# A four-layer graph network on one core: the last two products of sage_second as one of 256 columns

## The chip, the cores and the metric

The kernel runs on one core of a Trainium2 chip. Its time is the device time of one execution in microseconds (us). Three runs of the kernel before took 5426.86, 5427.26 and 5435.87 us; their median is 5427.26.

## The reference

The input is a graph of 50000 nodes with 128 features each and 100000 edges (25000 random ones in both directions, and a loop at each node). Four layers follow one another, each with a residual and a layer norm: a graph convolution, a three-layer GraphSAGE, an attention with a gated update, and a last convolution. The change touches the second and the third sum of GraphSAGE:

```python
def sage(h, w_self, w_neigh, b):
    agg = jax.ops.segment_sum(h[src], dst, num_segments=n) * inv_deg
    return h @ w_self + agg @ w_neigh + b
h = jax.nn.relu(sage(features, ws0, wn0, b0))
h = jax.nn.relu(sage(h, ws1, wn1, b1))
h = sage(h, ws2, wn2, b2)
```

All arrays are fp32. The last layer's mean over neighbours can be taken after the product with `wn2`, since both are linear. So the kernel multiplies the rows of the second layer's output with `ws2` and with `wn2` at once, stores the second product (128 features a node, table `t_v`) for the sums of the next stage, and the first one, with the residual, the bias and the node's own share added, in `r2`.

## The kernel before

The nodes are cut into 98 groups of 512 (four blocks of 128). Each stage of the network is a block of its own, with a barrier behind it, and goes once over all groups. In each stage every engine has a list of steps with a lag in groups (`over_groups`), so the order of an engine's instructions is written out by hand; the engines meet through semaphores. SP issues loads and stores, POOL the gathers of neighbours' rows. Per-edge sums are products with one-hot matrices.

In `sage_second` (lines 1695 to 1826) TensorE's order in each step is `sums` of one group, `across` of the group before it and `down` of the one before that. `sums` gives the neighbours' sums of 256 features in two banks of PSUM (helper line 910: short products, with the rows split into a high and a low part). `across` (line 1747) is the second layer: 16 products of 512 columns into banks 4 and 5, features on partitions. ScalarE's `relu` (line 1774) takes them to `hid`. `down` (line 1759) is the change's place: for each of the two weights, each of four blocks of 128 nodes and each half of the 256 features, one product with 128 rows of `hid` as the stationary operand and 128 columns of `wuv_s` as the moving one, so 32 products. `wuv_s` holds `ws2` in its columns 0 to 127 and `wn2` in columns 128 to 255. The product with `ws2` fills bank 6, block after block, that with `wn2` bank 7. Before `down` TensorE waits until both banks have been read for the group before (semaphores `kept` and `added`).

Behind `down`, ScalarE's `keep` (line 1783) copies bank 7 to `vout`, which SP stores in `t_v`. VectorE's `rest` adds bank 6 and the residual `xin` into `rout` (line 1811), adds the bias (line 1814), and then, when `kept` is there, four times `vout` times the node's own share (line 1821); SP stores `rout` in `r2`. In each step VectorE's order is: index copy for a later gather (`aim`, line 839), one-hots (874) and low parts (881), the neighbours' mean (1795, 1802), `rest`. ScalarE's order is: high parts (869), `relu`, `keep`.

`sage_first` (from line 1588) has a dense step like the new one: for each block one product of 256 columns with each of two weights, in turn, into the halves of a bank (lines 1631 and 1633), for each of four blocks, followed by eight transposes (1643).

Of the kernel before, what the change touches and what calls it, by code (L numbers as in the profile page):

```python
# [14 lines left out]
ALU = mybir.AluOpType  # L15
ACT = mybir.ActivationFunctionType
AX_X = mybir.AxisListType.X

P = 128
D = 128  # L20
HID = 256
NODES = 50000
EDGES = 100000
BLK = 4
# [160 lines left out]
def build_program(nc, x, src, dst, w1, b1, w2, b2, ws0, wn0, sb0, ws1, wn1, sb1, ws2, wn2, sb2,  # L185
# [66 lines left out]
    wuv_s = sb("wuv_s", [P, 2, HID])  # L252
# [15 lines left out]
    bank = [top.enter_context(nc.psum_tensor(f"bank{i}", [P, 512], F32)) for i in range(8)]  # L268
# [1426 lines left out]
    def sage_second():  # L1695


        with ExitStack() as ctx:
            ph = Phase(ctx, "s2")
            e = EdgeRows(ph, t_h, HID, split=True)  # L1700
            scale_row = ph.pair("scale", [P, GRP])
            xin = ph.pair("x", [P, GRP])
            ht, agg = ph.pair("ht", [P, 2, GRP], n=4), ph.pair("agg", [P, 2, GRP])
            hid = ph.pair("hid", [P, 2, GRP])
            vout, rout = ph.pair("vout", [P, GRP]), ph.pair("rout", [P, GRP])
            loaded, loaded_s, loaded_x = ph.sems("loaded", 4), ph.sems("loaded_s"), ph.sems("loaded_x")
            agged, link, link2 = ph.sem("agged"), ph.sem("link"), ph.sem("link2")
            hidden, relued, lowered = ph.sem("hidden"), ph.sem("relued"), ph.sem("lowered")
            kept, added, rested = ph.sem("kept"), ph.sem("added"), ph.sem("rested")
            st_v, st_r = ph.sems("stored_v"), ph.sems("stored_r")  # L1710
            block = ctx.enter_context(nc.Block())

            @block.gpsimd
            def _(pool):
                e.fetch(pool)

            @block.sync
            def _(sp):
                def loads(q):
                    load(sp, q, ht[q.r][:, :, :].rearrange("p h g -> p (h g)"), slab_of(htt, q.t), loaded[q.r],  # L1720
                         hidden, 4)
                    load(sp, q, scale_row[q.u][:, :], row_of(inv_d, q.t), loaded_s[q.u], agged)

                over_groups(sp, [
                    (0, loads),
                    (2, lambda q: load(sp, q, xin[q.u][:, :], own_group(t_x1, q.t), loaded_x[q.u],
                                       rested)),
                    (3, lambda q: store(sp, q, group_of(t_v[0:NPAD, :], q.t), vout[q.u][:, :], kept, st_v)),
                    (3, lambda q: store(sp, q, group_of(r2, q.t), rout[q.u][:, :], rested, st_r))])
                all_stored(sp, st_v, st_r)  # L1730

            @block.tensor
            def _(pe):
                def sums(q):
                    e.fetched(pe, q)
                    if not is_first(q.t):
                        pe.wait_ge(agged, q.t - 1)
                    e.sum_by_feature(pe, q, [bank[2 * q.u], bank[2 * q.u + 1]]).then_inc(e.summed, 1)

                def across(q):  # L1740
                    pe.wait_ge(agged, q.t + 1)
                    if not (isinstance(q.t, int) and q.t < 1):
                        pe.wait_ge(relued, q.t)
                    for o in range(2):
                        for k, (w, r) in enumerate(((ws1_s, ht[q.r]), (wn1_s, agg[q.u]))):
                            for h in range(2):
                                last = pe.matmul(bank[4 + o][:, :], w[:, h, o * P:(o + 1) * P], r[:, h, :],  # L1747
                                                 start=(k + h == 0), stop=(k + h == 2))
                    last.then_inc(hidden, 1)

                def down(q):
                    pe.wait_ge(relued, q.t + 1)
                    if not (isinstance(q.t, int) and q.t < 1):
                        pe.wait_ge(kept, q.t)
                        pe.wait_ge(added, q.t)
                    for w in range(2):
                        for b in range(BLK):
                            for h in range(2):
                                last = pe.matmul(bank[6 + w][:, b * D:(b + 1) * D],  # L1759
                                                 hid[q.u][:, h, b * P:(b + 1) * P],  # L1760
                                                 wuv_s[:, h, w * D:(w + 1) * D],
                                                 start=(h == 0), stop=(h == 1), skip_group_check=True)
                    last.then_inc(lowered, 1)

                over_groups(pe, [(1, sums), (2, across), (3, down)])

            @block.scalar
            def _(act):
                def relu(q):
                    act.wait_ge(hidden, q.t + 1)  # L1770
                    if not is_first(q.t):
                        act.wait_ge(lowered, q.t - 1)
                    for h in range(2):
                        last = act.activation(hid[q.u][:, h, :], bank[4 + h][:, :], ACT.Relu,  # L1774
                                              bias=sb1_c[:, h:h + 1])
                    last.then_inc(relued, 1)

                def keep(q):
                    act.wait_ge(lowered, q.t + 1)
                    if not is_first(q.t):  # L1780
                        act.wait_ge(st_v[q.u], q.n * 16)
                        act.wait_ge(rested, q.t - 1)
                    act.activation(vout[q.u][:, :], bank[7][:, :], ACT.Copy).then_inc(kept, 1)

                over_groups(act, [(0, lambda q: e.take_hi(act, q)), (2, relu), (3, keep)])

            @block.vector
            def _(dve):
                def mean(q):
                    dve.wait_ge(loaded[q.r], q.m * 16 + 16)  # L1790
                    dve.wait_ge(e.summed, q.t + 1)
                    if not is_first(q.t):
                        dve.wait_ge(hidden, q.t - 1)
                    for h in range(2):
                        last = dve.scalar_tensor_tensor(out=planes(agg[q.u][:, h, :]), in0=planes(ht[q.r][:, h, :]),
                                                        scalar=own[:, 0:1], in1=nodes(bank[2 * q.u + h]),
                                                        op0=ALU.mult, op1=ALU.add)
                    last.then_inc(link, 1)
                    dve.wait_ge(link, q.t + 1)
                    dve.wait_ge(loaded_s[q.u], q.n * 16 + 16)  # L1800
                    for h in range(2):
                        last = dve.tensor_tensor(agg[q.u][:, h, :], agg[q.u][:, h, :], scale_row[q.u][:, :],
                                                 ALU.mult)
                    last.then_inc(agged, 1)

                def rest(q):
                    dve.wait_ge(lowered, q.t + 1)
                    dve.wait_ge(loaded_x[q.u], q.n * 16 + 16)
                    if not is_first(q.t):
                        dve.wait_ge(st_r[q.u], q.n * 16)  # L1810
                    dve.tensor_tensor(rout[q.u][:, :], bank[6][:, :], xin[q.u][:, :], ALU.add)\  # L1811
                       .then_inc(added, 1)
                    dve.wait_ge(added, q.t + 1)
                    dve.tensor_tensor(rout[q.u][:, :], rout[q.u][:, :],
                                      sb2_r[:, :, :].rearrange("p b f -> p (b f)"), ALU.add)\
                       .then_inc(link2, 1)
                    dve.wait_ge(link2, q.t + 1)
                    dve.wait_ge(kept, q.t + 1)
                    for b in range(BLK):
                        f = slice(b * D, (b + 1) * D)  # L1820
                        last = dve.scalar_tensor_tensor(out=rout[q.u][:, f], in0=vout[q.u][:, f],
                                                        scalar=col(selfinv_n, q.t * BLK + b),
                                                        in1=rout[q.u][:, f], op0=ALU.mult, op1=ALU.add)
                    last.then_inc(rested, 1)

                e.on_vector(dve, [(0, lambda q: e.prepare_split(dve, q)), (1, mean), (3, rest)])


# [579 lines left out]
```

## Time and profile before

| what | us |
|---|---|
| median of three runs | 5427.26 |
| span of the profiled execution, first to last instruction | 5436.5 |
| TensorE's products busy | 4808.1 (88%) |
| VectorE busy | 3819.5 (70%) |
| ScalarE busy | 2699.8 (50%) |
| POOL busy | 3018.0 (56%) |
| `down`, busy time of 3136 products | 366.0 |

The profiled execution is known by its span alone: the page gives no time of it outside. Busy time of products is the time in which at least one is in flight; since they overlap, 3136 products of 275 ns each are busy for less than their sum. Shares are over all stages, and each stage has limits of its own.

### The profile page before, as it was taken

The numbers are of one execution on the slowest core, as the hardware profiler recorded it, in microseconds if no ns is written. First come the engines' busy times: TensorE is split into PE (matmuls) and PEld (weight loads), VectorE is DVE, ScalarE is ACT, GpSimd is POOL, SyncE is SP. The second block draws the span as 40 slices with busy tenths as digits, with TensorE's granted clock in tenths as the row PEclk, the third lists the DMA queues.
The fourth block names the chain that finished last, engine by engine and source line by source line (L and its number), as shares of the span: only waits on it lengthen the run. The fifth ranks groups of instructions, "written<-read, shape, count | busy, mean of one in ns | idle before, by whom it ended". The sixth has DMA issues, their size and how long they took to land. (4 is left out here: it accounts for less than half of the span.)

```text
span 5436.5 us, 107807 instructions
## 1 busy us (share of the span) xinstructions
PE 4808.1 (88%) x28685; PEld 3851.0 (71%) x28685; DVE 3819.5 (70%) x11588; ACT 2699.8 (50%) x6556; POOL 3018.0 (56%) x2962
## 2 busy tenths in 40 slices
PE   4499996777699989999999998899889999887888
PEld 4478885666689977777777776777656666787887
DVE  8567776776688865555555554788768888786776
ACT  2644444776444432222222221777777777574545
POOL 0077775777677744444443442777476665007776
PEclk9999998888799999999999998999999999999999
DMA  4889995666699985444544443788877777694555
GB/s 142 284 240 275 274 273 174 196 200 197 188 316 318 316 299 156 160 158 160 162 163 157 160 162 103 211 246 245 238 226 226 222 218 218 218 349 136 151 149 145
DMA packets 575803, 1145.78 MB, mean 211 GB/s; under 512 B 113731, under 2 KB 120938, under 8 KB 572586
## 3 DMA queue, kind: packets, MB, share of 16 engines
q1 hardware_dynamic: 475818, 924.99, 50.6%
q0 software_dynamic: 99840, 219.14, 16.5%
q8 instruction: 56, 0.92, 0.1%
q14 instruction: 89, 0.73, 0.0%
HBM read 705.69 MB, written 438.05 MB: 210 GB/s over the span
## 5 line engine op out<-in xcount | busy, mean ns | idle before, releaser
L846 POOL DMA_INDIRECT s_rows<-t_h,s_index x416 | 529.9, 1274 | 766.2 <-DVE s_index L839 664.9
L846 POOL DMA_INDIRECT g_rows<-t_x,g_index x416 | 425.6, 1023 | 385.5 <-issue 368.4
L846 POOL DMA_INDIRECT cb_rows<-t_x,cb_index x416 | 394.0, 947 | 395.7 <-DVE cb_index L839 271.3
L846 POOL DMA_INDIRECT at_rows<-t_m,at_index x416 | 433.1, 1041 | 305.4 <-DVE at_index L839 191.5
L846 POOL DMA_INDIRECT s_rows<-t_v,s_index x416 | 406.5, 977 | 207.4 <-issue 125.8
L1774 ACT ACTIVATE s_hid<-bank,sb_c 128x512 f32<-128x512 f32 x196 | 124.0, 683 | 787.7 <-PE bank L1747 787.7
L846 POOL DMA_INDIRECT s_rows<-t_x,s_index x416 | 419.9, 1009 | 166.9 <-issue 120.2
L846 POOL DMA_INDIRECT g_rows<-t_h,g_index x416 | 402.9, 969 | 171.0 <-issue 123.4
L910 PE MATMUL bank<-s_onehot,s_hi 128*128 128x80 f32 (+9 forms) x1758 | 438.2, 289 | 49.9 <-DVE s_lo L881 45.9
L1811 DVE TENSOR_TENSOR s_rout<-bank,s_x 128x512 f32<-128x512 f32 x98 | 67.7, 691 | 535.0 <-PE bank L1759 535.0
L910 PE MATMUL bank<-s_onehot,s_lo 128*128 128x80 f32 (+9 forms) x1758 | 431.7, 285 | 0.0
L910 PE MATMUL bank<-g_onehot,g_rows 128*128 128x80 f32 (+9 forms) x1172 | 287.9, 408 | 142.2 <-DMA g_rows<-t_h,g_index 132.8
L1759 PEld LDWEIGHTS bank<-wuv_s,s_hid 128*128 128x128 f32 x3136 | 365.5, 192 | 47.4 <-issue 47.4
L874 DVE TENSOR_SCALAR s_onehot<-iota,dcol 128x276 fp32r<-128x276 f32 (+15 forms) x1248 | 389.0, 374 | 0.5
L910 PEld LDWEIGHTS bank<-s_onehot,s_hi 128*128 128x128 f32 x1758 | 341.3, 194 | 55.1 <-issue 48.1
L1747 PE MATMUL bank<-s_ht,ws_s 128*128 128x512 f32 x784 | 375.5, 601 | 0.0
L910 PEld LDWEIGHTS bank<-g_onehot,g_rows 128*128 128x128 f32 x1172 | 240.1, 236 | 188.3 <-issue 109.6
L1747 PE MATMUL bank<-s_agg,wn_s 128*128 128x512 f32 x784 | 368.4, 592 | 0.0
L1759 PE MATMUL bank<-wuv_s,s_hid 128*128 128x128 f32 x3136 | 366.0, 275 | 0.9 <-DVE s_rout L1811 0.9
L910 PEld LDWEIGHTS bank<-s_onehot,s_lo 128*128 128x128 f32 x1758 | 341.9, 194 | 0.3 <-issue 0.2
L910 PE MATMUL bank<-cb_onehot,cb_rows 128*128 128x80 f32 (+9 forms) x1172 | 241.7, 360 | 91.1 <-DMA cb_rows<-t_x,cb_index 90.8
L910 PE MATMUL bank<-s_onehot,s_rows 128*128 128x80 f32 (+9 forms) x1172 | 240.0, 358 | 75.9 <-DMA s_rows<-t_v,s_index 68.7
(344 smaller groups left out, 13168.7 us busy)
## 6 DMA issues: line engine op xcount, KB each, us to landing
s_scale<-inv_d SPq DMA_DIRECT2D x196, 256.0 KB
t_h<-s_hout SPq DMA_DIRECT2D x98, 512.0 KB, 5.0
htt<-s_ht SPq DMA_DIRECT2D x98, 512.0 KB
s_ht<-htt SPq DMA_DIRECT2D x98, 512.0 KB
t_m<-s_mout SPq DMA_DIRECT2D x98, 264.0 KB
at_own<-t_m SPq DMA_DIRECT2D x98, 264.0 KB
t_x<-so_x SPq DMA_DIRECT2D x98, 256.0 KB, 4.6
g_own<-t_x SPq DMA_DIRECT2D x98, 256.0 KB
```

Of the source, the lines that this page charges most:

```text
L846: pool.indirect_dma_start(out=self.rows[:, self.ring(q) + k, :], out_offset=None, in_=self.table[0:NPAD, :], in_offset=bass.IndirectOffset ...
L874: last = dve.tensor_scalar(self.onehot[:, k, 0:WIDE[k]], iota[:, 0:WIDE[k]], col(dcol, q.m * K + k), None, ALU.is_equal)
L910: last = pe.matmul(to[:, a:b], part[:, at, h * P:(h + 1) * P], self.onehot[:, k, off:off + b - a], start=(i + s == 0), stop=(close and i + ...
L1747: last = pe.matmul(bank[4 + o][:, :], w[:, h, o * P:(o + 1) * P], r[:, h, :], start=(k + h == 0), stop=(k + h == 2))
L1759: last = pe.matmul(bank[6 + w][:, b * D:(b + 1) * D], hid[q.u][:, h, b * P:(b + 1) * P], wuv_s[:, h, w * D:(w + 1) * D], start=(h == 0), s ...
L1774: last = act.activation(hid[q.u][:, h, :], bank[4 + h][:, :], ACT.Relu, bias=sb1_c[:, h:h + 1])
L1811: dve.tensor_tensor(rout[q.u][:, :], bank[6][:, :], xin[q.u][:, :], ALU.add)\
```

## The change

`down` goes over blocks and halves only, and multiplies with all 256 columns of `wuv_s` at once: 16 products a group in place of 32. Bank 6 now holds blocks 0 and 1 (for each 128 columns of the first weight's product and 128 of the second's), bank 7 blocks 2 and 3. So both engines need both banks: ScalarE copies the second-weight halves, bank 6 first; VectorE adds the first-weight halves, bank 7 first. Two new semaphores keep them apart: each takes its second bank when the other has finished with it. All that follows in `rest` and the stores is as before.

```diff
+            def half_of(tile, i):
+                return tile[:, :].rearrange("p (b f) -> p b f", b=BLK)[:, 2 * i:2 * i + 2, :]
+            def lowered_half(i, w):
+                return bank[6 + i][:, :].rearrange("p (b f) -> p b f", f=HID)[:, :, w * D:(w + 1) * D]
...
-                    for w in range(2):
-                        for b in range(BLK):
-                            for h in range(2):
-                                last = pe.matmul(bank[6 + w][:, b * D:(b + 1) * D],
-                                                 hid[q.u][:, h, b * P:(b + 1) * P],
-                                                 wuv_s[:, h, w * D:(w + 1) * D],
-                                                 start=(h == 0), stop=(h == 1), skip_group_check=True)
+                    for b in range(BLK):
+                        for h in range(2):
+                            last = pe.matmul(bank[6 + b // 2][:, (b % 2) * HID:(b % 2 + 1) * HID],
+                                             hid[q.u][:, h, b * P:(b + 1) * P], wuv_s[:, h, :],
+                                             start=(h == 0), stop=(h == 1), skip_group_check=True)
...
-                    act.activation(vout[q.u][:, :], bank[7][:, :], ACT.Copy).then_inc(kept, 1)
+                    act.activation(half_of(vout[q.u], 0), lowered_half(0, 1), ACT.Copy).then_inc(kept_first, 1)
+                    act.wait_ge(added_first, q.t + 1)
+                    act.activation(half_of(vout[q.u], 1), lowered_half(1, 1), ACT.Copy).then_inc(kept, 1)
...
-                    dve.tensor_tensor(rout[q.u][:, :], bank[6][:, :], xin[q.u][:, :], ALU.add)\
+                    dve.tensor_tensor(half_of(rout[q.u], 1), lowered_half(1, 0), half_of(xin[q.u], 1), ALU.add)\
+                       .then_inc(added_first, 1)
+                    dve.wait_ge(kept_first, q.t + 1)
+                    dve.tensor_tensor(half_of(rout[q.u], 0), lowered_half(0, 0), half_of(xin[q.u], 0), ALU.add)\
                        .then_inc(added, 1)
```

## Rows read from the trace of the kernel before

**Rows 1.** Table of windows, all engines, middle of sage_second
```profile
core 0: us, PE busy (x) PEld busy (x) DVE busy (x) ACT busy (x) POOL busy (x), PEclk, DMA share, GB/s
2100.00:3300.00 1200.00, 1200.00 (x6512) 854.44 (x6511) 684.44 (x1472) 259.00 (x362) 486.90 (x377) 1.00 0.49 160
```

**Rows 2.** List of waits, same stretch: who waited for whom, us, times, longest
```profile
ACT s_hid L1774 <- PE bank L1747: 724.1, 90, 8.9
POOL s_rows L846 <- DVE s_index L839: 599.0, 89, 8.3
DVE s_rout L1811 <- PE bank L1759: 494.5, 91, 7.0
...
ACT s_vout L1783 <- PE bank L1759: 216.8, 91, 2.4
```

**Rows 3.** Groups by line and shape, TensorE: count | busy us, mean ns
```profile
L1747 PE MATMUL bank<-s_agg,wn_s 128*128 128x512 f32 x784 | 368.4, 592 | 0.0
L1759 PE MATMUL bank<-wuv_s,s_hid 128*128 128x128 f32 x3136 | 366.0, 275 | 0.9 <-DVE s_rout L1811 0.9
L1631 PE MATMUL bank<-ws_s,s_xt 128*128 128x256 f32 x784 | 239.7, 387 | 0.0
L1633 PE MATMUL bank<-wn_s,s_agg 128*128 128x256 f32 x784 | 233.2, 379 | 0.0
...
L1643 PE MATMUL bank<-ident,s_hout 128*128 128x128 f32 x784 | 101.9, 273 | 5.8 <-ACT s_ht L1663 5.8
```

**Rows 4.** Timeline, TensorE, sage_first: start us, us, engine, line
```profile
1702.59 0.68 PE L1631 MATMUL bank<-ws_s,s_xt 128*128 128x256 f32 x2
...
1703.54 0.59 PE L1631 MATMUL bank<-ws_s,s_xt 128*128 128x256 f32 x2
```

**Rows 5.** Timeline, TensorE, one group of sage_second; last row cut by the window
```profile
2599.85 1.88 PE L1747 MATMUL bank<-s_agg,wn_s 128*128 128x512 f32 x4
2601.57 3.73 PE L1759 MATMUL bank<-wuv_s,s_hid 128*128 128x128 f32 x32
2605.05 0.28 PE L910 MATMUL bank<-s_onehot,s_hi 128*128 128x80 f32 x1
...
2614.26 2.51 PE L1759 MATMUL bank<-wuv_s,s_hid 128*128 128x128 f32 x21
```

**Rows 6.** Timeline, VectorE and ScalarE behind that block
```profile
2605.34 0.69 DVE L1811 TENSOR_TENSOR s_rout<-bank,s_x 128x512 f32<-128x512 f32 x1 [6.72 <-PE bank L1759]
...
2605.47 0.60 ACT L1783 ACTIVATE s_vout<-bank 128x512 f32<-128x512 f32 x1 [2.44 <-PE bank L1759]
...
2605.97 1.27 ACT L869 ACTIVATE s_hi<-s_rows 128x1280 fp32r<-128x1280 f32 x1
...
2609.31 1.49 DVE L881 TENSOR_TENSOR s_lo<-s_rows,s_hi 128x1280 fp32r<-128x1280 f32 x1
```

**Rows 7.** Groups by line and shape: shorter reads of PSUM by both engines
```profile
L1963 DVE TENSOR_TENSOR s_mout<-bank,bm_r 128x264 f32<-128x264 f32 x196 | 80.9, 420 | 0.0
...
L1917 ACT ACTIVATE s_scaled<-bank,inv_n 128x128 f32<-128x128 f32 x392 | 111.5, 377 | 0.0
```

**Rows 8.** Timeline, a hand-over from ScalarE to VectorE, start of sage_second
```profile
2061.65 0.84 ACT L869 ACTIVATE s_hi<-s_rows 128x768 fp32r<-128x768 f32 x1
...
2062.53 0.96 DVE L881 TENSOR_TENSOR s_lo<-s_rows,s_hi 128x768 fp32r<-128x768 f32 x1 [6.16 <-ACT s_hi L869]
```

**Rows 9.** Timeline, the end of sage_second
```profile
3340.66 3.73 PE L1759 MATMUL bank<-wuv_s,s_hid 128*128 128x128 f32 x32
...
3344.43 0.69 DVE L1811 TENSOR_TENSOR s_rout<-bank,s_x 128x512 f32<-128x512 f32 x1 [7.85 <-PE bank L1759]
...
3345.27 3.81 PE L1759 MATMUL bank<-wuv_s,s_hid 128*128 128x128 f32 x32 [0.88 <-DVE s_rout L1811]
...
3350.57 1.14 DVE L1821 SCALAR_TENSOR_TENSOR s_rout<-s_vout,selfinv_n,s_rout 128x128 f32<-128x128 f32 x4
...
3351.74 0.33 SPq L1038 DMA_DIRECT2D r<-s_rout  x1
```

More of the change, by code:

```diff
@@ L1710, in sage_second @@
             st_v, st_r = ph.sems("stored_v"), ph.sems("stored_r")
+            kept_first, added_first = ph.sem("kept_first"), ph.sem("added_first")
             block = ctx.enter_context(nc.Block())
+            def half_of(tile, i):
+                return tile[:, :].rearrange("p (b f) -> p b f", b=BLK)[:, 2 * i:2 * i + 2, :]
+            def lowered_half(i, w):
+                return bank[6 + i][:, :].rearrange("p (b f) -> p b f", f=HID)[:, :, w * D:(w + 1) * D]
             @block.gpsimd
```

## The prediction

> **What bounds the kernel now.** I read the table of windows first, because a change inside one stage is worth only what that stage makes of it. Over 1200 us in the middle of sage_second TensorE is busy in all of them, at a granted clock of 1.00, its full 2.4 GHz level; VectorE is at 57%, ScalarE at 22%, the DMA share is 0.49 [rows 1]. The list of waits for the same stretch comes second, and what is to be seen in it is who is missing: TensorE waits for nobody. ScalarE waits for TensorE before the relu (724.1 us) and before its PSUM copy (216.8), VectorE before its add (494.5), and POOL waits for VectorE's index [rows 2]. So the stage is as long as TensorE's products follow one another, and everything else has room. Shorter products there shorten the kernel one for one, until another engine's room is used up; longer work elsewhere costs nothing while it fits into that room.
>
> Busy times cannot price a product, because products overlap. I take the spacing instead, from groups whose members follow without a gap: the busy time of one block is (n - 1) spacings and one duration. For the products that the change replaces: 366.0 us / 98 blocks = 3.735; less one duration of 0.275, over 31, gives 0.1116 us. For products of 256 columns, which sage_first issues in pairs: 233.2 / 392 pairs = 0.5949; less 0.379 gives 0.2159. For 512 columns, in fours: 368.4 / 196 = 1.880; less 0.592, over 3, gives 0.4292. For the transposes of 128 columns, in eights: 101.9 / 98 = 1.040; less 0.273, over 7, gives 0.1095 [rows 3]. Twice 0.1116 is 0.2232, more than 0.2159, so 128 columns are a little dear here. That is all the change can win on TensorE.
>
> **The products.** Removed are 32 products of 128 columns a group, 32 x 0.1116 = 3.571 us; added are 16 of 256 columns, 16 x 0.2159 = 3.454. The number of columns streamed stays, half of the weight loads go. The saving is 0.117 us a group and, over 98 groups, 11.5 us, all on the path, since the block stands between products on both sides with no idle time [rows 5]. What the trace does not show is a 256-column product in this place. The nearest rows are the pair in sage_first: fp32 as here, activations as the stationary operand, a weight matrix as the moving one, and a new weight load for each product. I take that value. From below it is bounded by half of the 512-column spacing, 0.2146, which would save 0.137 us a group, 13.5 us in all; from above by twice today's spacing, 0.2232, which saves nothing. The line L1631 has a longer busy time than L1633 (239.7 against 233.2): its first pair behind the short products of the sums takes 0.68 us, the next one 0.59 [rows 4]. In sage_second the block follows products of 512 columns [rows 5], so I do not count that.
>
> The trace has 0.1095 us for a transpose of 128 columns and 0.1116 for a product [rows 3]; I read the 2.1 ns between them as the weight load, which is as wide as the stream and is not quite hidden behind it. The Trainium skill speaks against this reading: in TensorE: Matmul & The Clock Gate, Back-to-back issue gap, a product alone costs its columns at 2.4 GHz and a fixed 2.5 ns or so, so that fewer and wider products save only that fixed part; 16 x 2.5 ns x 98 would be an estimate of 3.9 us by that page, in place of 11.5. The same section says that a stream of loads and products is set by both, which is what the rows show here.
>
> **The two engines behind the block.** Before, VectorE adds all of bank 6 in 0.69 us while ScalarE copies all of bank 7 in 0.60, side by side [rows 6]. After, each takes its half of one bank, waits for the other, and takes the other bank. Neither half is in the trace. For VectorE's 256 columns out of PSUM the nearest row is 264 columns at 0.42 us; bounds are 0.35 (half of 0.69) and 0.69. ScalarE's lies between 0.377 (128 columns from PSUM) and 0.60 (512); a straight line through these gives 0.45 [rows 6, 7]. Bounds for the hand-over between the engines: ScalarE ended at 2062.49 and the waiting VectorE began at 2062.53, so 0.04 us [rows 8]; VectorE to TensorE took 0.15 (3345.12 to 3345.27) [rows 9]. ScalarE begins 0.13 us after VectorE [rows 6], so: 0.13 + 0.45 + 0.04 + 0.42 = 1.04 us in place of 0.69. VectorE's add ends 0.35 us later, at the bounds 0.15 to 0.75 later; ScalarE's copy also ends at about 1.04, which is 0.3 later than its 0.73.
>
> What is queued behind the two new waits? On VectorE the second add, the bias add, the four multiply-adds, and then for later groups the index copy, the one-hots, the low parts and the mean; on ScalarE the second copy, the high parts and the relu. Their customers are TensorE (through the low parts and the mean), POOL (through the index) and SP's two stores. In the steady state I cost all of it at nothing, and this is the cover: TensorE needs both copies done only at its next block, which starts at 2614.26, while they are done at 2606.07 [rows 5, 6]: 8 us of room. VectorE stands idle for 494.5 / 91 = 5.4 us a group before its add [rows 2], so its queue is level again before the next one. ScalarE's high parts end at 2607.24 and VectorE takes them up at 2609.31 [rows 6], 2 us of room, and both move by about the same. If this cover were gone, each group would pay 0.35 us, or 34 us, three times the gain.
>
> **The end of the stage** has no cover. The last two blocks follow each other directly: the second waited 0.88 us for VectorE's add, and behind the last one nothing but the add, the bias, the multiply-adds and the store is left [rows 9]. So the longer exchange is paid twice: 2 x 0.35 = 0.7 us (0.3 to 1.5). The next stage starts behind a barrier, as before.
>
> **Sum.** 11.5 - 0.7 = 10.8 us. The profiled execution has a span of 5436.5 us, and the page has nothing of it that lies outside; it is 9.2 us above the median of the three runs, 5427.26, and near the slowest of them. As a difference in a stage with a steady clock the sum carries over: 5425.7 for an execution like the profiled one, and 5416.5 on the median, which I forecast. That is 0.20% less. A measurement of this kernel can tell some 0.2%, 10.9 us, from no change, so the forecast stands on that line.
>
> **Rivals.**
> A, only a fixed cost per product goes. If the 2.1 ns over the transposes belong to this place and not to the load, the new spacing is 0.2159 + 2 x 0.0021 = 0.2201, and the gain 16 x (0.2232 - 0.2201) x 98 = 4.9 us, less 0.7: 5423.1. For it: the transposes, also at 128 columns with loads of their own, are at 0.1095. Against: the pair in sage_first has the same kind of operands. 8%. The Trainium skill's Back-to-back issue gap, cited above, is a rule of this kind.
> B, no gain at all: the wide product takes twice the narrow one, and the end is paid: 5428.0. For it: the columns are the same. Against: 0.2159 and 0.4292 in the rows. 5%.
> C, slower: the exchange becomes what TensorE waits for. Its place is VectorE's queue, and it decides from 5.4 us a group on; 6 us would cost (6 - 5.4 - 0.1) x 98, some 50 us: 5476. For it: VectorE now waits for ScalarE and ScalarE for VectorE, so that a late store or a late load of one stops both. Against: halves of half a microsecond, and a room ten times as large. 3%.
> D, the spacing falls to half of the 512-column one: 13.5 - 0.7 = 12.8 us, 5414.5. 4%.
>
> **How the numbers follow.** The forecast as described has 80%, A 8, B 5, D 4, C 3. The forecast is 0.1 us on the near side of the line, and the three runs shown are 9 us apart, so I give 42 of its 80 to faster, 38 to the same. Faster: 42 + 4 = 46%. Same: 38 + 8 + 5 = 51%. Slower: 3%. The range takes in D with 4 us below it for the runs' spread, and above the forecast A and the spread of the three runs (5416.5 + 9): 5410 to 5427. Left out are C, most of B and some of the spread.
>
> **What would show it.** The block as one row of 16 products over 15 x 0.2159 + 0.379 = 3.62 us, in place of 3.73; one of 3.69 would be A. From the first block's start to the last one's end 11 us less. TensorE still busy in all of the stage, VectorE's idle time before its first half about 0.5 us a group shorter, the last block's wait 1.2 in place of 0.88. Idle time on TensorE in the middle of the stage, or a clock below 1.00 there, would make the forecast wrong; so would a stage that is 11 us shorter with the time given back in another.

## The result: slower, by a stage that the change does not touch

The changed kernel takes 5447.03 us (median of five runs, 5446.1 to 5452.35), against 5427.26 before: a ratio of 1.0038, with a 95% interval of 1.0027 to 1.0049. I had forecast 5416.5 and a range of 5410 to 5427; "slower" had 3%, all of it for rival C. The profiled execution has a span of 5444.4 us and took 5446.22.

The stage that is changed did what was forecast. The group of the wide products, TensorE, by line and shape (count | busy us, mean ns | idle before), then the windows row of the same stretch as in [rows 1]:

```profile
L1765 PE MATMUL bank<-wuv_s,s_hid 128*128 128x256 f32 x1568 | 354.5, 379 | 1.0 <-DVE s_rout L1821 1.0
```

```profile
2100.00:3300.00 1200.00, 1200.00 (x5102) 812.44 (x5102) 701.61 (x1567) 274.43 (x456) 484.25 (x376) 1.00 0.49 161
```

One block is 354.5 / 98 = 3.617 us (forecast 3.62), so the spacing is (3.617 - 0.379) / 15 = 0.2159, the very number of sage_first's pair [rows 3]. TensorE is still busy all the time at its full clock.

A word on the counts. The profile shows each of these fp32 products as two records: the loops of the code issue 2 x 4 x 2 = 16 products a group before and 8 now, and the rows have 3136 / 98 = 32 and 1568 / 98 = 16. What the prediction counts as a product is such a record, and its prices are those of records, so its sum is not touched.

The line of the products, before (first) and after (second), with the minimum, median and longest duration in ns and the first and last start in us:

```profile
L1759 PE MATMUL bank<-wuv_s,s_hid x3136: 272/275/347, 2070.6 to 3348.8; 128*128 128x128 f32 x196
```

```profile
L1765 PE MATMUL bank<-wuv_s,s_hid x1568: 379/379/454, 2063.9 to 3330.5; 128*128 128x256 f32 x196
```

From the first start to the last there were 1278.2 us before, and there are 1266.6 now, so 11.6 us less; forecast were 11.5 with a small loss at the end. The exchange and the end of the stage, as in [rows 6] and [rows 9], from the timelines of VectorE, ScalarE and TensorE:

```profile
2602.72 3.62 PE L1765 MATMUL bank<-wuv_s,s_hid 128*128 128x256 f32 x16
...
2606.37 0.42 DVE L1818 TENSOR_TENSOR s_rout<-bank,s_x 128x256 f32<-128x256 f32 x1 [4.19 <-PE bank L1765]
2606.79 0.42 DVE L1821 TENSOR_TENSOR s_rout<-bank,s_x 128x256 f32<-128x256 f32 x1
...
2606.37 0.39 ACT L1788 ACTIVATE s_vout<-bank 128x256 f32<-128x256 f32 x1 [2.19 <-PE bank L1765]
2606.83 0.39 ACT L1790 ACTIVATE s_vout<-bank 128x256 f32<-128x256 f32 x1
...
3327.16 3.69 PE L1765 MATMUL bank<-wuv_s,s_hid 128*128 128x256 f32 x16 [1.02 <-DVE s_rout L1821]
```

Both engines begin together and their halves are 0.42 and 0.39 us, so nobody waits long for the other: the add is over 0.84 us after its start in place of 0.69, and the wait of the last block is 1.02 in place of 0.88. That last block takes 3.69 us, but it is no sign of rival A: it starts behind a wait, as the last block before did (3.81 in place of 3.73 [rows 9]), and the blocks in the stream take 3.62.

So where does the loss come from? The line of a product that sage_third issues once a group has the stage's extent, before (first) and after (second):

```profile
L1892 PE MATMUL bank<-s_xt,whh_s x196: 592/592/931, 3422.5 to 3933.0; 128*128 128x512 f32 x196
```

```profile
L1902 PE MATMUL bank<-s_xt,whh_s x196: 592/592/1142, 3402.7 to 3940.5; 128*128 128x512 f32 x196
```

510.5 us became 537.8, so 27.3 more, in the stage behind the changed one. Its code is the same. VectorE's waits in that stage (us in total, times, longest) show what is new; before, the list has no issue wait above 0.2 us:

```profile
DVE s_index L839 <- issue: 35.9, 7, 6.0
...
DVE s_mout L1973 <- issue: 13.1, 9, 2.4
```

"Issue" means that VectorE waited for nothing that the profile knows. The timeline of VectorE around one such wait, after, and the same place in a turn before:

```profile
3586.58 0.81 DVE L874 TENSOR_SCALAR s_onehot<-iota,dcol 128x252 f32<-128x252 f32 x3
3592.49 0.17 DVE L839 COPY s_index<-idx 128x5 uint32 x1 [5.09 <-issue]
...
3593.18 0.15 DVE L1971 COPY s_asks<-bank 128x2 f32<-128x2 f32 x1
3595.48 0.43 DVE L1973 TENSOR_TENSOR s_mout<-bank,bm_r 128x264 f32<-128x264 f32 x1 [2.15 <-issue]
```

```profile
3597.50 0.81 DVE L874 TENSOR_SCALAR s_onehot<-iota,dcol 128x252 f32<-128x252 f32 x3
3598.40 0.17 DVE L839 COPY s_index<-idx 128x5 uint32 x1
```

The wait stands where the loop jumps back to its start, once in eight groups. What it does to TensorE is seen one turn earlier, in the same products ahead of the wait and behind it:

```profile
3538.95 1.06 PE L1907 MATMUL bank<-wm_s,s_xt 128*128 128x132 f32 x8
...
3547.68 2.13 PE L1907 MATMUL bank<-wm_s,s_xt 128*128 128x132 f32 x8 [4.29 <-DVE s_mout L1973]
```

TensorE waited 4.29 us for VectorE, and behind that its products took twice as long: the granted clock is 0.50 from 3548 to 3552, its 1.2 GHz level. The windows of the stage, before (first) and after:

```profile
3422.00:3933.00 511.00, 456.72 (x2754) 377.37 (x2753) 419.63 (x1926) 400.33 (x1112) 355.96 (x365) 0.98 0.84 242
```

```profile
3402.00:3940.00 538.00, 466.35 (x2755) 385.43 (x2753) 417.69 (x1927) 400.13 (x1109) 354.61 (x365) 0.95 0.78 230
```

So of 27.0 us TensorE stands idle for 17.4 more (71.65 in place of 54.28), and its products are 9.6 longer, at a mean granted clock of 0.95 in place of 0.98.

And the DMA table of the stage (packets, MB, share) has more instruction packets, before (first) and after:

```profile
q14 instruction: 14, 0.11, 0.1%
```

```profile
q14 instruction: 54, 0.44, 0.2%
```

Forty more packets of 0.44 MB / 54 = 8.1 KB. The loop of this stage makes nine turns, so it jumps back eight times, and there are five packets to each jump; from 3500 to 3860, inside the loop, the queue has 37 packets after and none before. VectorE seems to fetch its loop anew in each turn. Theory F is that the change moved this loop. It gives VectorE one instruction more a group, 18 in the whole program (two ahead of sage_second's loop, eight in it, eight behind), so all that follows stands 18 places further on. Rival T is that sage_third suffers from the new timing of sage_second and its stores.

### The profile page after: what moved, and what is told of

It reads as the page before. It is cut to its first block and busy times, and to the rows that moved or that the text cites. A ratio compares the mean times of both kernels' runs of the same rounds, so it can differ in the third digit from the quotient of the medians.

```text
span 5444.4 us, 104867 instructions
## 1 busy us (share of the span) xinstructions
PE 4807.6 (88%) x27117; PEld 3809.2 (70%) x27117; DVE 3830.2 (70%) x11686; ACT 2717.0 (50%) x6654; POOL 3021.2 (55%) x2962
## 5 line engine op out<-in xcount | busy, mean ns | idle before, releaser
L1818 DVE TENSOR_TENSOR s_rout<-bank,s_x 128x256 f32<-128x256 f32 x98 | 41.6, 424 | 503.2 <-PE bank L1765 503.2
L1765 PEld LDWEIGHTS bank<-wuv_s,s_hid 128*128 128x128 f32 x1568 | 297.8, 190 | 83.2 <-issue 47.8
L1765 PE MATMUL bank<-wuv_s,s_hid 128*128 128x256 f32 x1568 | 354.5, 379 | 1.0 <-DVE s_rout L1821 1.0
```

The lines of the kernel that those rows point to most:

```text
L1765: last = pe.matmul(bank[6 + b // 2][:, (b % 2) * HID:(b % 2 + 1) * HID], hid[q.u][:, h, b * P:(b + 1) * P], wuv_s[:, h, :], start=(h == 0) ...
L1818: dve.tensor_tensor(half_of(rout[q.u], 1), lowered_half(1, 0), half_of(xin[q.u], 1), ALU.add)\
```

## The experiments

### The changed kernel, its later VectorE code moved on

```diff
+                if table is t_v:
+                    for i in range(40):
+                        dve.memset(unused[:, i:i + 1], 0.0)
```

This stands in `general_sums`, between sage_second and sage_third, in a branch that is not taken (the tile `unused` is made beside it).

> The changed kernel, with 40 one-column memsets put into VectorE's program between sage_second and sage_third, in a branch that these inputs jump over: nothing of it runs, it only moves the place of VectorE's loop in sage_third by 40 instructions. Theory F (instruction fetch: the 18 instructions that the change adds to VectorE's program moved that loop across a boundary of its fetched pieces, and each of its turns now waits for them): the idle time put down to issue before the index copy (35.9 us in 7) goes, the instruction packets on queue 14 in sage_third fall from 54 to about 14, sage_third is some 25 us shorter, and the kernel takes 5427.3 - 10.8 = 5416, within 5 us. Rival T (timing: the shorter sage_second or the longer exchange leaves sage_third's loads and stores in a worse order): nothing changes, 5447.

5416.34 us (11 runs, 5410.58 to 5422.41); the ratio to the kernel before, which took 5427.73 beside it (29 runs), is 0.998, 0.9971 to 0.9989. The extent of sage_third and the stage's instruction packets:

```profile
L1906 PE MATMUL bank<-s_xt,whh_s x196: 592/592/1087, 3402.0 to 3908.9; 128*128 128x512 f32 x196
```

```profile
q14 instruction: 14, 0.11, 0.1%
```

The stage is 506.9 us again, 30.9 shorter than after the change, the kernel 30.7 (5447.03 was measured on another occasion, beside a kernel before of 5427.26). Nothing that runs was changed, so T has fallen. The time is what the prediction gave to the change itself.

### The kernel before, moved on by 18

```diff
+                if table is t_v:
+                    for i in range(18):
+                        dve.memset(unused[:, i:i + 1], 0.0)
```

> The kernel before, with 18 one-column memsets in the same branch that is jumped over, so that VectorE's loop in sage_third stands where the change put it; ScalarE's and TensorE's programs are as before. Theory F: sage_second as before, sage_third with some 50 instruction packets on queue 14 and an issue wait of VectorE once a turn, some 25 us longer; 5427 + 25 = 5452, at least 5445. Rival T, or a shift in ScalarE's program (18 instructions there too) as the cause: 5427, as before.

5458.11 us (5453.26 to 5459.15), a ratio of 1.0058, 1.0045 to 1.0072. VectorE's waits in sage_third and the packets:

```profile
DVE s_index L839 <- issue: 35.9, 8, 5.1
DVE s_mout L1967 <- issue: 15.7, 9, 2.4
```

```profile
q14 instruction: 54, 0.44, 0.3%
```

The same two waits, at the same two statements, in the kernel before: 18 instructions that never run cost 30.4 us (5458.11 - 5427.73). ScalarE's program, which the change also lengthens by 18, was not moved here, and was moved in the run above without harm; so it is VectorE's.

### The exchange without the wide product

```diff
+                    for b in range(BLK):
+                        for w in range(2):
+                            for h in range(2):
+                                f = (b % 2) * HID + w * D
+                                last = pe.matmul(bank[6 + b // 2][:, f:f + D], hid[q.u][:, h, b * P:(b + 1) * P],
+                                                 wuv_s[:, h, w * D:(w + 1) * D],
...
```

The 40 memsets of the first experiment are in this kernel, too.

> The changed kernel with its exchange, but with 32 products of 128 columns a group (each weight by itself, into the new places of the two banks), and with the 40 memsets that are jumped over. If the exchange costs only what the end of the stage shows, and the gain is the wide product's alone: 5427.3 + 0.7 = 5428, TensorE busy in all of sage_second, one block 3.73 us. If the exchange is what made the change slow: 5440 or more.

5426.53 us (10 runs), a ratio of 1.0001, 0.9992 to 1.001. The extent of its products and one of its blocks:

```profile
L1771 PE MATMUL bank<-wuv_s,s_hid x3136: 272/275/348, 2056.0 to 3334.4; 128*128 128x128 f32 x196
```

```profile
2599.74 3.73 PE L1771 MATMUL bank<-wuv_s,s_hid 128*128 128x128 f32 x32
```

1278.4 us, 0.2 more than before. In the steady state the exchange is free, as its cover said; the gain is the wide product's.

### The wide product without the exchange

```diff
+    both = top.enter_context(nc.psum_tensor("both", [P, 1024], F32))
+    bank += [both[:, 0:512], both[:, 512:1024]]
...
-                    act.wait_ge(lowered, q.t + 1)
+                    act.wait_ge(added, q.t + 1)
...
+                    act.activation(by_block(vout[q.u]), product(1), ACT.Copy).then_inc(kept, 1)
...
+                    dve.tensor_tensor(by_block(rout[q.u]), product(0), by_block(xin[q.u]), ALU.add)\
+                       .then_inc(added, 1)
```

`product(w)` is the 512 columns of weight `w` in both banks; ScalarE copies after VectorE's add.

> The wide product with no exchange: banks 6 and 7 are one tile of 1024 columns, VectorE adds its 512 columns out of both banks in one instruction, and ScalarE then copies its 512 in one; no engine has an instruction more than before, so VectorE's loop in sage_third stands where it stood. Theory F: sage_second some 11 us shorter, sage_third as before; the copy ends some 0.7 us later than in the kernel before, paid twice at the end of the stage: 5427.3 - 11.5 + 1.4 = 5417. Rival T (a shorter sage_second slows sage_third): 5440 to 5447.

5417.28 us (12 runs), a ratio of 0.9981, 0.9973 to 0.999. Its last block and the two engines before it:

```profile
3328.36 0.69 DVE L1817 TENSOR_TENSOR s_rout<-both,s_x 128x512 f32<-128x512 f32 x1 [7.73 <-PE both L1766]
...
3329.09 0.60 ACT L1789 ACTIVATE s_vout<-both 128x512 f32<-128x512 f32 x1 [2.91 <-DVE s_rout L1817]
...
3329.79 3.69 PE L1766 MATMUL both<-wuv_s,s_hid 128*128 128x256 f32 x16 [1.46 <-ACT s_vout L1789]
```

One after the other costs 0.58 us more at the last block than the kernel before has (1.46 against 0.88); from the first product's start to the last one's it takes 1267.0 us, 0.4 more than the change. It needs no filling, because no program grows. It and the first experiment cannot be told apart; both beat the kernel before, by 0.2%, and the change.

### Four more places, to find the edges

The kernel before with 9, 25, 34 and 46 such memsets, one run each, beside one run of the kernel before at 5433.19.

> The kernel before with 9 memsets that are jumped over in place of 18: where is the edge? VectorE's loop in sage_third has 283 instructions a turn, and a fetched piece of 8192 bytes holds 128 of them at 64 bytes each. If what matters is the number of pieces that the loop touches (three or four), a bad place is 26 or 27 positions wide out of 128, and the kernel before (0) and the changed one (18) lie on the two sides of one edge. 9 halves the distance: with the profile's packets on queue 14 in sage_third some 14 it lies above 9, with some 50 below. No verdict on theory F hangs on this run.

> 25 memsets that are jumped over. By the count of pieces every place from 18 to 25 is bad whichever side of 9 the edge is on, since the bad stretch is 26 or 27 wide and begins after 0: some 50 instruction packets in sage_third, 5450 to 5460. If only the distance matters (a longer program, more to fetch), 25 is a little worse than 18.

> 34 memsets that are jumped over. By the count of pieces it is bad if the edge lies from 8 up to 18, and good again, as the kernel before, if it lies from 1 to 7; so it must agree with the run of 9: bad here if 9 is good.

> 46 memsets that are jumped over. By the count of pieces the place is good again whichever edge it is (at most 18 + 27 = 45): some 14 instruction packets in sage_third and 5427, within 8 us. If a longer VectorE program were the cause and not its place, this would be the slowest of the four, 5458 or more.

| moved on by | kernel, us | instruction packets in sage_third | issue wait at the loop's start, us |
|---|---|---|---|
| 9 | 5459.95 | 54 | 46.5 |
| 25 | 5477.44 | 54 | 60.9 |
| 34 | 5429.32 | 14 | none |
| 46 | 5425.15 | 14 | none |

With 0 (good) and 18 (bad) that is one bad stretch, and behind it the time is as before: the place matters, not the length of the program. The run of 25 missed its expectation of 5450 to 5460: a bad place does not have one price. With 9 and with 25 VectorE has no second wait; the one of 25 is the longest:

```profile
DVE s_index L839 <- issue: 60.9, 8, 8.9
```

A count fits all six. A turn of VectorE's loop has 283 instructions in the built program. The Trainium skill (Runtime: NRT & Kernel Launch, Instruction fetch mechanics) has blocks of 16 KiB for 256 instructions, so 64 bytes each; the packets here are 8.1 KB, half of the block that the page has, and the measured size decides; from it and the page's 64 bytes I estimate 128 instructions a packet. 283 is 2 x 128 + 27, so the loop touches three pieces from 102 starting places and four from the other 26. It starts at instruction 2894 of the built program before, at place 2894 - 22 x 128 = 78 and some unknown c for what is loaded ahead of it. Place 78 + c is good, 87, 96 and 103 + c are bad, 112 and 124 + c good: all true if c is 16 to 23. So is the changed kernel with 40, good at 96 + 40 = 136 + c. In the built program's own terms the loop stood 1 to 8 instructions short of the first bad place before the change, and 10 to 17 past it after.

The second wait bears the count out. After the change, and with 18, it stands before the second add into `mout`, which is the tenth instruction of the loop; if a piece ends there, 96 + c + 9 = 128, and c is 23, inside the range. With 25 the same border then lies two instructions behind the loop's start, ahead of the index copy, and the second wait falls together with the first; with 9 it lies 18 behind, and no wait is seen there. This is an argument from one loop: a loop of another length was not tried, the fifth packet of a turn is one more than the four pieces of the count, and why 25 costs more than 9 and 18 beyond this stays open.

The same section of the Trainium skill says that crossing a block in sequence is mostly hidden, and that a taken branch to a place outside the pages held forces a fetch before the engine goes on. The trace agrees with the second: in the bad places a wait stands at the jump back, 4.5 to 7.6 us a turn (35.9 / 8 to 60.9 / 8). With the first it agrees in the good places, which have no issue wait at the jump; but the second wait of the change, 13.1 us in nine, stands behind the jump, where the loop runs on in sequence, and is not hidden. How many pieces are held, and why a fetch takes so long here, no run shows; that VectorE's pieces are those on queue 14 is read from the counts of packets, which come and go with its waits at the jump in every run.

## Why the prediction was wrong

Its sum was right and its border was too narrow.
- The products: 11.5 us forecast, 11.6 measured over the blocks; A, B and D (4.9, 0 and 13.5) have fallen. The 2.1 ns over the transposes do not belong to this place; whether they went with the weight load or with the product no run tells, since both were halved. (By A's own spacing its block would have been 15 x 0.2201 + 0.379 = 3.68 and not 3.69.)
- The exchange: I took 0.35 us a group, hidden, and 0.7 at the end. It is 0.15, hidden, and some 0.3 at the end: ScalarE began with VectorE and not 0.13 later, and its half took 0.39 and not 0.45. The bounds of 0.15 to 0.75 do not follow from the terms beside them, which give 0.13 + 0.377 + 0.04 + 0.35 - 0.69 = 0.21 and 0.13 + 0.60 + 0.04 + 0.69 - 0.69 = 0.77; that 0.15 was met is luck.
- The cover: TensorE without idle time, exchange alone at a ratio of 1.0001. Rival C did not happen.
- The failed step is the sentence that closes the part on the end of the stage: "The next stage starts behind a barrier, as before." It was taken to mean that nothing of the change reaches over the barrier. The change counted as products of TensorE and, for VectorE and ScalarE, as durations; that one more instruction a group also moves all code behind it was in no part of the sum. Its price is 30.7 us (5447.03 - 5416.34), nearly three times the gain: VectorE's waits for its code, TensorE's idle time behind them, and the lower clock behind that. The last sentence of the prediction named the sign, time given back in another stage, without a mechanism or a chance.
- The page of before could have warned: its row of q14 with 89 instruction packets (131 after) shows that programs are fetched piece by piece, though not that this loop stood so close to a border.

## What to carry to other kernels

When an edit adds or removes instructions in an engine's program, compare the later stages, too: an issue wait at the start of a loop, once a turn, with more instruction packets, points to the place of the code and not to what the edit computes. Move the loop with instructions in a branch that isn't taken before judging the edit, or find a form of it that adds none. And price a product by its spacing in a full stream: that gave the gain to a tenth of a microsecond over the 98 groups.

## What the runs showed of the hardware

Eighteen instructions that are jumped over cost 30 us (five runs against 29), 25 of them 5477.44 - 5433.19 = 44 us in a single run against a single run, and 46 nothing that one run shows; the 29 runs of the kernel before spread over 23 us. In the stage that pays, TensorE's granted clock fell to its 1.2 GHz level behind a wait of 4.29 us, and the same eight records took 2.13 us in place of 1.06. A copy of 256 columns from PSUM, in two runs of 128 with a gap, takes ScalarE 0.39 us, against 0.60 for 512 and 0.377 for 128 with a scale: the shorter copy is cheaper than a straight line through those two, which join a copy with a scale to one without. Records of fp32 products of 256 columns, two to a product and each with a weight load, follow one another at 0.2159 us in two different stages, those of 128 columns at 0.1116.
